# A ternary feed-forward layer whose down projection runs two tiles behind, with f32 transposes in a ring of three buffers

## The chip, the cores and the metric

The kernel runs on one core of one Trainium2 chip. The metric is the device time of the whole kernel in microseconds (us). The core has five engines that run side by side: PE (TensorE, matmuls; its weight loads are listed apart as PEld), DVE (VectorE), ACT (ScalarE), POOL (GpSimd) and SP (SyncE, which here only starts transfers). Each runs its own instructions in the order in which they are written and waits for others by semaphores. PE has two clock levels, 1.2 and 2.4 GHz; the profile gives the granted clock as a share of full speed.

## What is computed

Four layers, each added to x, on 2048 rows of 512 numbers: a masked attention, a ternary feed-forward layer, a second attention and a gated feed-forward layer. The change lies in the second:

```python
def _rmsnorm(x, g):
    return g * (x * jax.lax.rsqrt(jnp.mean(x * x, axis=-1, keepdims=True) + EPS))
def _act_quant(x):
    scale = 127.0 / jnp.clip(jnp.max(jnp.abs(x), axis=-1, keepdims=True), 0.0001, None)
    y = jnp.clip(jnp.round(x * scale), -128, 127) / scale
...
def _linear_bit(x, w, g):
    xq = _act_quant(_rmsnorm(x, g))
    wq = _ternary_quant(w)
    return jnp.einsum('bsd,od->bso', xq, wq)
swish = jax.nn.silu(_linear_bit(x, w1, g1))
x_v = _linear_bit(x, w2, g2)
h = swish * x_v
return _linear_bit(h, w3, g3)
...
x = x + _L0_ffn_ref(_layernorm(x, axis=-1), L0_ffn_w1, ...)
```

w1 and w2 lead from 512 to 2048 columns, w3 from 2048 back to 512.

## The kernel before

`build_ternary_ffn` starts at line 743. The three ternary matrices lie in SBUF in bf16 from the start of the stage. The 2048 rows are cut into 16 tiles of 128 (NT). The work on a tile has these parts, by the names in the code:

- **prepare** (DVE, lines 931 to 944): mean and variance of the tile's rows (`bn`, `mv`), `u` = (x - mean) times g1 and times g2, and the largest value of each (`amax`). POOL turns these into the scale factors `kx` and `dqx` in a chain of eleven small instructions (lines 844 to 862), each of which waits for the one before.
- **quantise** (line 946): DVE multiplies and rounds `u` by adding a large constant (`um`), takes the constant off again and writes bf16 (`xq`); PE transposes the eight 128x128 blocks into PSUM (`TX`, line 1024), ACT copies them to SBUF (`xqt`, line 894).
- **products** (PE, lines 1030 to 1040): for n from 0 to 3 four matmuls of 512 columns into `G` (w1) and four into `V` (w2), both with two buffers in PSUM. ACT takes silu of G (line 914), DVE multiplies it by V to `h` (`gate`, line 969), ACT squares and sums h (line 901), POOL multiplies h by g3 to `u3` (line 871), DVE takes its largest value (line 974). Then DVE reduces the four partial results (`red`) and POOL makes `k3` and `dq3` of them (lines 876 to 883).
- **h rounded** (ACT, line 907): one instruction over 2048 columns (`hm`); DVE writes it as bf16 (`hq`, line 985), PE transposes 16 blocks into `TH` (line 1046), ACT copies one half and DVE the other to `hqt` (lines 921 and 1004).
- **down** (PE, line 1057): 16 matmuls with w3 into `DN`; DVE scales them and adds them to x (`xr`, line 1011); SP stores the tile.

The order is written out by hand in `step(t, before, ahead)` on each engine. Step t does the products of tile t, the transposes and the down matmuls of tile t-1 (`before`), the quantise of tile t+1 and the prepare of tile t+2 (`ahead`). Steps 1 to 13 are one hardware loop (`Fori`), whose waits compare with register values. x is loaded twice per tile: into `xz` for prepare and into `xr` for the update, each a single buffer.

## Time and profile before

| | us |
|---|---|
| median of 3 runs | 1853.65 (1852.92 to 1854.41) |
| the profiled execution, its own time | 1850.29 |
| its span, first to last instruction | 1848.5 |
| ternary stage, first instruction to the next stage's first | 650.88 to 975.42 |

| engine | busy us of the span | share |
|---|---|---|
| PE | 1489.4 | 81% |
| DVE | 959.9 | 52% |
| ACT | 678.6 | 37% |
| POOL | 404.6 | 22% |

These shares are means over four stages with different limits, so they say little about the ternary stage. For that the profile is read by stretches of time (windows), by the timeline of one step, and by groups of equal instructions. In a timeline row the bracket gives how long the engine stood idle before the instruction and whose result ended that. The rows stand below, ahead of the prediction.

### The profile page before, as it was taken

The numbers are of one execution on the slowest core, as the hardware profiler recorded it, in microseconds if no ns is written. First come the engines' busy times: TensorE is split into PE (matmuls) and PEld (weight loads), VectorE is DVE, ScalarE is ACT, GpSimd is POOL, SyncE is SP. The second block draws the span as 40 slices with busy tenths as digits, with TensorE's granted clock in tenths as the row PEclk, the third lists the DMA queues.
The fourth block names the chain that finished last, engine by engine and source line by source line (L and its number), as shares of the span: only waits on it lengthen the run. The fifth ranks groups of instructions, "written<-read, shape, count | busy, mean of one in ns | idle before, by whom it ended". The sixth has DMA issues, their size and how long they took to land. (4 is left out here: it accounts for less than half of the span.)

```text
span 1848.5 us, 25537 instructions
## 1 busy us (share of the span) xinstructions
PE 1489.4 (81%) x9033; PEld 657.7 (36%) x9106; DVE 959.9 (52%) x1526; ACT 678.6 (37%) x1212; POOL 404.6 (22%) x502
## 2 busy tenths in 40 slices
PE   3568878877787747867672898899599999999998
PEld 2334534444343213333330122222144444444443
DVE  6544744646646358788853788888332032131220
ACT  2153444444434424544440566666322021121120
POOL 4210101101100046666642233342200000000000
PEclk8678988889888968888885899999799999999999
DMA  5524254253442121111113556453300100100100
GB/s 137 91 87 107 81 142 87 96 127 81 122 97 72 58 66 34 45 40 41 44 35 120 164 180 217 150 194 117 124 1 0 69 1 1 68 0 0 46 0 23
DMA packets 91704, 146.29 MB, mean 79 GB/s; under 512 B 7624, under 2 KB 48136, under 8 KB 90064
## 3 DMA queue, kind: packets, MB, share of 16 engines
q1 hardware_dynamic: 78816, 119.93, 22.9%
q10 hardware_dynamic: 12800, 25.17, 4.3%
q8 instruction: 58, 0.95, 0.2%
q14 instruction: 30, 0.25, 0.0%
HBM read 114.23 MB, written 30.83 MB: 78 GB/s over the span
## 5 line engine op out<-in xcount | busy, mean ns | idle before, releaser
L488 DVE TENSOR_REDUCE a_negmax<-a_psX 128x4 f32<-128x1024 f32 x128 | 149.8, 1216 | 170.9 <-PE a_psX L682 170.3
L1349 DVE TENSOR_REDUCE c_negmax<-c_psA 128x1 f32<-128x512 f32 x256 | 163.9, 673 | 60.4 <-PE c_psA L1420 58.2
L373 ACT ACTIVATE a_probs<-a_psB 128x512 f32<-128x512 f32 x256 | 138.5, 593 | 145.6 <-PE a_psB L692 145.5
L1653 PE MATMUL d_psGU<-d_zt_lo,last_w_hi 128*128 128x512 bf16 x501 | 189.9, 379 | 2.2 <-DVE d_zt_lo L1607 1.7
L1653 PE MATMUL d_psGU<-d_zt_hi,last_w_hi 128*128 128x512 bf16 x502 | 190.3, 379 | 0.6
L1653 PE MATMUL d_psGU<-d_zt_hi,last_w_lo 128*128 128x512 bf16 x501 | 189.9, 379 | 0.6
L1576 ACT ACTIVATE d_silu<-d_psGU 128x512 f32<-128x512 f32 x64 | 38.2, 597 | 378.2 <-PE d_psGU L1653 378.2
L692 PE MATMUL a_psB<-a_qs,a_ks 115*128 115x256 bf16 x512 | 138.7, 401 | 45.7 <-ACT a_probs L373 40.2
L1295 ACT ACTIVATE c_probs<-c_psB 128x512 f32<-128x512 f32 x256 | 142.2, 595 | 90.8 <-PE c_psB L1433 88.6
L1618 DVE TENSOR_TENSOR d_h<-d_psGU,d_silu 128x512 f32<-128x512 f32 x64 | 44.2, 691 | 236.4 <-PE d_psGU L1653 236.4
L1420 PE MATMUL c_psA<-c_ks,c_qs 96*128 96x512 bf16 x256 | 105.1, 412 | 50.6 <-DMA c_qs<-q_scr 29.1
L1057 PE MATMUL b_psD<-ternary,b_hq_t 128*128 128x512 bf16 x254 | 85.9, 513 | 53.0 <-ACT b_hq_t L921 53.0
L682 PE MATMUL a_psX<-a_ks,a_qs 113*128 113x256 bf16 x512 | 79.9, 297 | 52.3 <-DVE a_negmax L488 29.8
L1433 PE MATMUL c_psB<-c_qs,c_ks 98*128 98x512 bf16 x256 | 95.0, 389 | 7.7 <-ACT c_probs L1295 7.0
L1663 PE MATMUL d_psD<-last_w_hi,d_h_lo 128*128 128x512 bf16 x252 | 95.5, 379 | 0.3
L1663 PE MATMUL d_psD<-last_w_hi,d_h_hi 128*128 128x512 bf16 x251 | 95.1, 379 | 0.4
L1663 PE MATMUL d_psD<-last_w_lo,d_h_hi 128*128 128x512 bf16 x249 | 94.4, 379 | 0.2
L266 POOL TENSOR_SCALAR a_ve<-a_mv 128x2 f32<-128x2 f32 x8 | 1.9, 232 | 418.1 <-DVE a_mv L421 418.1
L871 POOL TENSOR_TENSOR b_u<-b_h,b_g 128x512 f32<-128x512 f32 x64 | 84.4, 1333 | 40.6 <-DVE b_h L969 37.5
L1630 DVE TENSOR_TENSOR d_xr<-d_psD,d_xr 128x512 f32<-128x512 f32 x16 | 10.4, 690 | 150.6 <-PE d_psD L1663 113.2
L692 PEld LDWEIGHTS a_psB<-a_qs,a_ks 115*128 115x128 bf16 x512 | 43.6, 107 | 125.8 <-ACT a_probs L373 74.9
L705 PE MATMUL a_psOS<-a_probs,a_v 128*32 128x256 f32 x1024 | 85.7, 462 | 0.0
(207 smaller groups left out, 2641.9 us busy)
## 6 DMA issues: line engine op xcount, KB each, us to landing
a_tern_stage<-in_w ACTq DMA_DIRECT2D x32, 768.0 KB, 7.5
c_weight_stage<-in_w_last SPq DMA_DIRECT2D x8, 1536.0 KB, 8.7
a_ks<-k_scr SPq DMA_DIRECT2D x24, 256.0 KB
a_qs<-q_scr SPq DMA_DIRECT2D x24, 256.0 KB
c_ks<-k_scr SPq DMA_DIRECT2D x48, 128.0 KB, 2.6
c_qs<-q_scr SPq DMA_DIRECT2D x48, 128.0 KB, 3.0
a_xz<-in_x SPq DMA_DIRECT2D x8, 512.0 KB, 18.5
a_ctx<-in_ctx_t SPq DMA_DIRECT2D x8, 512.0 KB, 12.7
```

What stands on the lines that cost most here:

```text
L373: act.activation(pr[:, e % 4, :, jj * P:(jj + 1) * P].rearrange("p r (a i) -> p a r i", a=2), B[:, u % 2, :].rearrange("p (a r i) -> p a r ...
L488: v.tensor_reduce(negm[:, u, :], X[:, 2 * (u % 2):2 * (u % 2) + 2, :].rearrange("p a (j k) -> p (a j) k", k=SEQ), AX.X, ALU.max, negate=Tr ...
L692: last = pe.matmul(B[:, u % 2, a * SEQ:(a + 1) * SEQ], ks[par][0:K_ALL, j, grp, kt * P:(kt + 1) * P], qflat[par][0:K_ALL, SHARE * grp * SE ...
L705: pe.matmul(OS[32 * r:32 * r + 32, c % 2, 0, :], v1[par][:, kt, grp, :], pr[:, (2 * grp + kt) % 4, r, :], start=(grp % 2 == 0 and kt == 0) ...
L871: g.tensor_tensor(u3[:, n, :], h[:, n, :], g3[:, n * 512:(n + 1) * 512], ALU.mult)\
L1057: last = pe.matmul(DN[:], hqt[:, i, :], w3[:, i, :], start=(i == 0), stop=(i == FC - 1))
L1295: act.activation(pr[:, e % 2, j, :], B[:, j % 2, :], ACT.Exp, scale=HD1 ** -0.5)\
L1349: v.tensor_reduce(negm[:, u:u + 1], A[:, u % 2, :], AX.X, ALU.max, negate=True)\
L1420: pe.matmul(A[:, u % 2, :], qs[par][0:K1, head, (u % QT) * P:(u % QT + 1) * P], ks[par][0:K1, head, :], start=True, stop=True).then_inc(s[ ...
L1433: pe.matmul(B[:, j % 2, :], ks[par][0:K1 + 2, head, kt * P:(kt + 1) * P], qs[par][0:K1 + 2, head, :], start=True, stop=True).then_inc(s["s ...
L1653: last = pe.matmul(GU[:, 2 * up + i % 2, :], wgu[wh][:, k, o:o + P], zt[zh][:, k, :], start=(k == 0 and j == 0), stop=(k == DC - 1 and j = ...
L1663: last = pe.matmul(DN[:, t, :], ht[hh][:, i, t * P:(t + 1) * P], wd[wh][:, i, :], start=(i == 0 and j == 0), stop=(i == FC - 1 and j == 2))
```

## The change

All of it is in `build_ternary_ffn`.

- The down matmuls of a tile come two steps after its products instead of one, in four groups of four that stand between the product groups. Step t does products of t, transposes and down of t-2.
- There is no bf16 copy before a transpose. ACT rounds x (`rounded`) and h (`scaled`, in two halves of 1024 columns); PE transposes the f32 values with the large constant still on them, four blocks into one PSUM bank of 512 f32. Three such banks (`T`) form a ring for the chunks of tiles t-2 (four of h) and t+1 (two of x) in the order `CHUNKS`. The constant is taken off where a chunk is read out (`take`): even chunks by ACT, odd ones by DVE with a tensor-scalar instruction.
- x has one ring of ten tiles (`b_x`) that serves prepare and update, so each tile is loaded once. SP loads tiles 0 and 1 ahead of g1 and g2, and waits for a store's landing before it loads the tile ten further on.
- prepare runs four tiles ahead in rings of four; `u` for g1 and g2 is one instruction of 1024 columns, and so is `amax`. POOL makes `kx` and `dqx` for two tiles at once, 13 instructions in every even step, in four parts between its products with g3.
- DVE takes the largest values of u3 in two reduces of 1024 columns instead of four of 512.
- `dqx_now` and `dq3_now`, the two small copies, are gone. The hardware loop is gone too: 19 steps are written out, with constant waits.

The diff, cut to its core:

```diff
     NF = FF // 512
+    RING, RU = 10, 4
+
+
+    CHUNKS = [("x", 0, 0), ("x", 0, 1)]
+    for t in range(NT + 2):
+        CHUNKS += [("h", t - 2, i) for i in range(2) if t >= 2]
+        CHUNKS += [("x", t + 1, j) for j in range(2) if t + 1 < NT]
+        CHUNKS += [("h", t - 2, i) for i in range(2, NF) if t >= 2]
+    AT = {c: k for k, c in enumerate(CHUNKS)}
+    TAKEN = {c: (c[2] % 2, sum(1 for d in CHUNKS[:k + 1] if d[2] % 2 == c[2] % 2)) for k, c in enumerate(CHUNKS)}
...
+            def rounded(t):
+                act.wait_ge(s["kx_done"], 2 * (t // 2 + 1))
+                act.wait_ge(s["u_done"], t + 1)
+                if t >= 2:
+                    act.wait_ge(s["filled"], AT["x", t - 2, 1] + 1)
+                for j in range(2):
+                    act.activation(um[:, t % 2, j, :], u[:, t % RU, j, :], ACT.Identity, scale=kx[:, t % RU, j:j + 1],
+                                   bias=keep["round"][:]).then_inc(s["um_done"], 1)
+
+            def take(kind, t, i):
+                if (kind, t, i) not in AT:
+                    return
+                act.wait_ge(s["filled"], AT[kind, t, i] + 1)
+                dst = xqt[:, t % 2, i, :] if kind == "x" else hqt[:, t % 2, i * 512:(i + 1) * 512]
+                act.activation(dst, T[:, AT[kind, t, i] % 3, :], ACT.Identity, bias=unround[:]).then_inc(s["taken_act"], 1)
...
+            def scaled(t, half):
+                if half == 0:
+                    act.wait_ge(s["k3_done"], 2 * (t + 1))
+                    act.wait_ge(s["u3_done"], NF * (t + 1))
+                    if t >= 2:
+                        act.wait_ge(s["filled"], AT["h", t - 2, NF - 1] + 1)
+                own = slice(half * FF // 2, (half + 1) * FF // 2)
+                act.activation(hm[:, t % 2, own], u3[:, t % 2].rearrange("p n d -> p (n d)")[:, own], ACT.Identity,
+                               scale=k3[:, t % 2:t % 2 + 1], bias=keep["round"][:]).then_inc(s["hm_done"], 1)
+
+            act.wait_ge(s["init"], 2)
+            rounded(0)
+            take("x", 0, 0)
+            for t in range(NT + 2):
+                now = t < NT
+                if now:
+                    gate(t, 0)
+                take("h", t - 2, 0)
+                if t + 1 < NT:
+                    rounded(t + 1)
+                if now:
+                    squares(t, 0)
+                    gate(t, 1)
+                    squares(t, 1)
+                    gate(t, 2)
+                take("x", t + 1, 0)
+                if 1 <= t <= NT:
+                    scaled(t - 1, 0)
+                if now:
+                    squares(t, 2)
+                    gate(t, 3)
+                take("h", t - 2, 2)
+                if 1 <= t <= NT:
+                    scaled(t - 1, 1)
+                if now:
+                    squares(t, 3)
...
-            def quantise(t):
-                dve.wait_ge(s["kx_done"], t + 1)
-                for j in range(2):
-                    v.tensor_scalar(um[:, j, :], u[:, j, :], kx[:, j:j + 1], ROUND, ALU.mult, ALU.add)\
-                        .then_inc(s["xq_rounded"], 1)
-                need(dve, s["tx_done"], t)
-                for j in range(2):
-                    dve.wait_ge(s["xq_rounded"], 2 * t + j + 1)
-                    v.tensor_scalar(xq[:, j, :], um[:, j, :], ROUND, 127.0, ALU.subtract, ALU.min)\
-                        .then_inc(s["xq_done"], 1)
...
+            for t in range(NT + 3):
+                now = t < NT
+                ahead = prepare(t + 4) if t + 4 < NT else iter(())
+                if t >= 3:
+                    update(t - 3)
+                if now:
+                    gate(t, 0)
+                if 1 <= t <= NT:
+                    largest(t - 1, 1)
+                    reduced(t - 1)
+                next(ahead, None)
+                if now:
+                    gate(t, 1)
+                take("h", t - 2, 1)
+                next(ahead, None)
+                if now:
+                    gate(t, 2)
+                take("x", t + 1, 1)
+                next(ahead, None)
+                if now:
+                    largest(t, 0)
+                    gate(t, 3)
+                take("h", t - 2, 3)
 
...
+            def transposed(kind, t, i):
+                if (kind, t, i) not in AT:
+                    return
+                k = AT[kind, t, i]
+                if k >= 3:
+                    engine, count = TAKEN[CHUNKS[k - 3]]
+                    pe.wait_ge(taken[engine], count)
+                if kind == "x":
+                    pe.wait_ge(s["um_done"], 2 * t + i + 1)
+                    src = um[:, t % 2, i, :]
+                else:
+                    pe.wait_ge(s["hm_done"], 2 * t + i // 2 + 1)
+                    src = hm[:, t % 2, i * 512:(i + 1) * 512]
+                for c in range(DC):
+                    last = pe.transpose(T[:, k % 3, c * P:(c + 1) * P], src[:, c * P:(c + 1) * P], keep["ident"][:])
+                last.then_inc(s["filled"], 1)
...
+            def down(t, i):
+                if ("h", t, i) not in AT:
+                    return
+                engine, count = TAKEN["h", t, i]
+                pe.wait_ge(taken[engine], count)
+                if i == 0:
+                    need(pe, s["x_updated"], t)
+                for k in range(4 * i, 4 * i + 4):
+                    last = pe.matmul(DN[:], hqt[:, t % 2, k * P:(k + 1) * P], w3[:, k, :], start=(k == 0), stop=(k == FC - 1))
+                if i == NF - 1:
                     last.then_inc(s["d_done"], 1)
 
...
+            for t in range(NT + 2):
+                for n in range(NF):
+                    if t < NT:
+                        product(t, n, 0, G, "silu_done", "g_done")
+                        product(t, n, 1, V, "h_done", "v_done")
+                    if n:
+                        down(t - 2, n - 1)
+                    transposed("h", t - 2, n)
+                    if n == 1:
+                        for j in range(2):
+                            transposed("x", t + 1, j)
+                down(t - 2, NF - 1)
 
 
```

PE before, from the transposes of h in the loop's body to the end of the body (`psTH` and `psTX` are the two transposes, `psD` the down matmuls, in brackets what a row waits for):

```order
L1046 MATMUL b_psTH<-ident_bf,b_hq 128x128 [waits b_hqt_dve,b_hqt_act]
L1046 MATMUL b_psTH<-ident_bf,b_hq 128x128 x15
L1020 ISA
L1024 MATMUL b_psTX<-ident_bf,b_xq 128x128 [waits b_xqt_done,b_xq_done]
L1024 MATMUL b_psTX<-ident_bf,b_xq 128x128 x7
L1057 MATMUL b_psD<-ternary,b_hq_t 128x512 [waits b_x_updated,b_hqt_act]
L1057 MATMUL b_psD<-ternary,b_hq_t 128x512 x7
L1057 MATMUL b_psD<-ternary,b_hq_t 128x512 [waits b_hqt_dve]
L1057 MATMUL b_psD<-ternary,b_hq_t 128x512 x7
```

PE after, the second half of a steady step and the first groups of the next:

```order
L1114 MATMUL b_psD<-ternary,b_hq_t 128x512 [waits b_taken_act]
L1114 MATMUL b_psD<-ternary,b_hq_t 128x512 x3
L1093 MATMUL b_psT<-ident,b_h_rounded 128x128 [waits b_hm_done,b_taken_act]
L1093 MATMUL b_psT<-ident,b_h_rounded 128x128 x3
L1114 MATMUL b_psD<-ternary,b_hq_t 128x512 [waits b_taken_dve]
L1114 MATMUL b_psD<-ternary,b_hq_t 128x512 x3
L1102 MATMUL b_psG<-ternary,b_xq_t 128x512 [waits b_silu_done,b_taken_act]
L1102 MATMUL b_psG<-ternary,b_xq_t 128x512 x3
L1102 MATMUL b_psV<-ternary,b_xq_t 128x512 [waits b_h_done,b_taken_dve]
L1102 MATMUL b_psV<-ternary,b_xq_t 128x512 x3
```

Where all 16 transposes of h, the 8 of x and the 16 down matmuls stood in a row at the end, groups of four now stand between the products; the last down group stands directly behind the last transposes of h, and the one before it behind the last V group.

ACT before, one turn of the loop's body:

```order
L907 ACTIVATE b_h_rounded<-b_u3,round_bias,b_k3 128x2048
L914 ACTIVATE b_silu<-b_psG,b_dqx_now 128x512 x2
L901 ACTIVATE b_sq,b_ssq<-b_h 128x512
L914 ACTIVATE b_silu<-b_psG,b_dqx_now 128x512
L901 ACTIVATE b_sq,b_ssq<-b_h 128x512
L914 ACTIVATE b_silu<-b_psG,b_dqx_now 128x512
L901 ACTIVATE b_sq,b_ssq<-b_h 128x512 x2
L921 ACTIVATE b_hq_t<-b_psTH 128x1024
L894 ACTIVATE b_xq_t<-b_psTX 128x1024
```

ACT after, the end of one steady step and the start of the next (it begins with silu of n = 2):

```order
L932 ACTIVATE b_silu<-b_psG,b_dqx 128x512
L927 ACTIVATE b_xq_t<-b_psT,b_minus_round 128x512
L950 ACTIVATE b_h_rounded<-b_u3,round_bias,b_k3 128x1024
L940 ACTIVATE b_sq,b_ssq<-b_h 128x512
L932 ACTIVATE b_silu<-b_psG,b_dqx 128x512
L927 ACTIVATE b_hq_t<-b_psT,b_minus_round 128x512
L950 ACTIVATE b_h_rounded<-b_u3,round_bias,b_k3 128x1024
L940 ACTIVATE b_sq,b_ssq<-b_h 128x512
L932 ACTIVATE b_silu<-b_psG,b_dqx 128x512
L927 ACTIVATE b_hq_t<-b_psT,b_minus_round 128x512
L919 ACTIVATE b_u_rounded<-b_u,round_bias,b_kx 128x512 x2
L940 ACTIVATE b_sq,b_ssq<-b_h 128x512
```

ACT has gained the two roundings of x, three takes of 512 columns stand where two copies of 1024 were, and the rounding of h is split and stands among the squares; the take of h's chunk 2 is behind silu of n = 3.

## Rows read from the trace of the kernel before

**Rows 1.** Windows of the ternary stage: stretch, its length, busy us per engine (instructions), clock, DMA.
```profile
core 0: us, PE busy (x) PEld busy (x) DVE busy (x) ACT busy (x) POOL busy (x), PEclk, DMA share, GB/s
...
650.88:670.13 19.25, 1.04 (x8) 0.77 (x8) 7.17 (x15) 1.02 (x1) 5.74 (x14) 0.50 0.32 110
...
705.72:948.14 242.42, 180.53 (x923) 84.67 (x935) 193.30 (x319) 121.78 (x196) 156.52 (x270) 0.87 0.14 41
...
948.14:975.42 27.28, 18.13 (x95) 8.86 (x94) 11.85 (x20) 9.32 (x15) 7.99 (x10) 0.87 0.14 49
```

**Rows 2.** Timeline, one steady step: start, length, engine, line, operation, out<-in [idle before <-releaser].
```profile
819.14 0.69 ACT L914 ACTIVATE b_silu<-b_psG,b_dqx_now 128x512 f32<-128x512 f32 x1 [0.46 <-DVE b_dqx_now L961]
...
820.11 0.75 DVE L969 SCALAR_TENSOR_TENSOR b_h<-b_psV,b_dqx_now,b_silu 128x512 f32<-128x512 f32 x1 [1.16 <-ACT b_silu L914]
...
820.55 0.69 ACT L914 ACTIVATE b_silu<-b_psG,b_dqx_now 128x512 f32<-128x512 f32 x1 [0.72 <-PE b_psG L1033]
...
821.13 0.62 ACT L901 ACTIVATE b_sq<-b_h 128x512 f32<-128x512 f32 x1
...
821.65 0.19 ACT L901 ACTIVATION_READ_ACCUMULATOR b_sq<-b_h 128x1 f32 x1
...
824.66 1.06 PE L1046 MATMUL b_psTH<-ident_bf,b_hq 128*128 128x128 bf16 x16
...
826.52 0.62 PE L1024 MATMUL b_psTX<-ident_bf,b_xq 128*128 128x128 bf16 x8 [0.80 <-DVE b_xq L954]
...
827.75 0.63 ACT L901 ACTIVATE b_sq<-b_h 128x512 f32<-128x512 f32 x1 [3.06 <-DVE b_h L969]
...
830.69 5.03 PE L1057 MATMUL b_psD<-ternary,b_hq_t 128*128 128x512 bf16 x16 [3.55 <-ACT b_hq_t L921]
```

**Rows 3.** Groups by line and form, ternary stage: count | busy us, mean ns | idle before.
```profile
L969 DVE SCALAR_TENSOR_TENSOR b_h<-b_psV,b_dqx_now,b_silu 128x512 f32<-128x512 f32 x64 | 47.5, 742 | 22.2 <-ACT b_silu L914 20.0 <-PE b_psV L1038 2.2
...
L907 ACT ACTIVATE b_h_rounded<-b_u,round_bias,b_k 128x2048 f32<-128x2048 f32 x16 | 33.5, 2093 | 55.7 <-POOL b_dq L883 55.7
...
L871 POOL TENSOR_TENSOR b_u<-b_h,b_g 128x512 f32<-128x512 f32 x64 | 84.4, 1333 | 40.6 <-DVE b_h L969 37.5 <-issue 2.9
...
L939 DVE SCALAR_TENSOR_TENSOR b_u<-b_xz,b_mv,b_g 128x512 f32<-128x512 f32 x32 | 22.6, 749 | 0.6
...
L985 DVE TENSOR_SCALAR b_hq<-b_h_rounded 128x2048 bf16<-128x2048 f32 x16 | 19.5, 1217 | 0.6 <-ACT b_h_rounded L907 0.6
```

**Rows 4.** Timeline of PE in the last stage: f32 transposes, then bf16 matmuls.
```profile
1675.48 1.94 PE L1642 MATMUL d_psGU<-ident,d_z 128*128 128x128 f32 x16 [0.88 <-DVE d_h L1618]
1677.25 0.38 PE L1663 MATMUL d_psD<-last_w_hi,d_h_hi 128*128 128x512 bf16 x1
1677.47 0.38 PE L1663 MATMUL d_psD<-last_w_hi,d_h_lo 128*128 128x512 bf16 x1
```

**Rows 5.** Groups by line and form, whole span: nearest forms to the new instructions.
```profile
L488 DVE TENSOR_REDUCE a_negmax<-a_psX 128x4 f32<-128x1024 f32 x128 | 149.8, 1216 | 170.9 <-PE a_psX L682 170.3
...
L1571 ACT ACTIVATE d_h_hi<-d_h 128x512 bf16<-128x512 f32 x64 | 39.8, 622 | 8.8 <-DVE d_h L1618 8.8
...
L1564 ACT ACTIVATE d_zt_hi<-d_psGU 128x512 bf16<-128x512 f32 x16 | 8.5, 602 | 23.2 <-PE d_psGU L1642 22.8
...
L1270 ACT ACTIVATE c_ctx_hi<-c_ctx 128x1024 bf16<-128x1024 f32 x8 | 8.4, 1056 | 31.7 <-DMA c_ctx<-in_ctx 24.9 <-DMA k_scr<-c_ctx_lo 6.8
```

**Rows 6.** Windows after a stop of PE, and without one (columns as in 1).
```profile
830.69:834.40 3.71, 3.71 (x11) 1.42 (x12) 3.43 (x9) 0.86 (x1) 1.96 (x4) 0.61 0.00 0
...
955.90:957.75 1.85, 0.00 (x2) 0.12 (x3) 1.12 (x2) 1.56 (x3) 1.25 (x1) 1.00 0.00 0
...
967.12:969.90 2.78, 2.78 (x7) 1.04 (x8) 0.00 (x0) 0.00 (x0) 0.00 (x0) 0.50 0.00 0
```

**Rows 7.** Timeline of POOL: first and last link of an undisturbed h chain.
```profile
958.28 0.19 POOL L876 TENSOR_SCALAR b_scalars<-b_red 128x1 f32<-128x1 f32 x1 [1.13 <-DVE b_red L1001]
...
960.48 0.19 POOL L883 TENSOR_TENSOR b_dq<-b_scalars,level 128x1 f32<-128x1 f32 x1
```

**Rows 8.** Timeline of DVE: the first tile of the stage.
```profile
660.17 0.69 DVE L934 BATCH_NORM_STATS2 b_bn<-b_xz 128x6 f32<-128x512 f32 x1 [20.33 <-DMA b_xz<-x]
```

More of the change, by code:

```diff
@@ L789, in build_ternary_ffn @@
         s = {n: ctx.enter_context(nc.semaphore("b_" + n)) for n in names}
+        loaded = [s[f"x_loaded{i}"] for i in range(4)]
+        taken = [s["taken_act"], s["taken_dve"]]
         block = ctx.enter_context(nc.Block())
@@ L836, in _ @@
+            for t in range(4, RING):
+                load(t)
+            for t in range(NT):
+                sp.wait_ge(s["x_updated"], t + 1)
+                sp.dma_start(x_out[t * P:(t + 1) * P, :], xt[:, t % RING, :]).then_inc(s["stored"], DMA)
+                if t + RING < NT:
+                    sp.wait_ge(s["stored"], (t + 1) * DMA)
+                    load(t + RING)
             sp.wait_ge(s["stored"], NT * DMA)
@@ L890, in _ @@
+            pool.wait_ge(s["g3_loaded"], DMA)
+            for t in range(NT + 1):
+                chain = iter(())
+                if t % 2 == 0 and t + 2 < NT:
+                    chain = x_chain(t + 2)
+                if t >= 1:
+                    h_chain(t - 1)
+                if t < NT:
+                    for n in range(NF):
+                        gated(t, n)
+                        next(chain, None)
         @block.scalar
         def _(act):
-            def quantise(t):
-                act.wait_ge(s["tx_done"], t + 1)
-                act.activation(xqt[:], TX[:], ACT.Copy).then_inc(s["xqt_done"], 1)
@@ new lines, in prepare @@
+                yield
+                dve.wait_ge(s["mv_done"], t + 1)
+                if t == 0:
+                    dve.wait_ge(s["g12_loaded"], 2 * DMA)
+                v.scalar_tensor_tensor(out=u[:, r], in0=xt[:, t % RING, :].rearrange("p (o d) -> p o d", o=1)
+                                       .broadcast_to([P, 2, D]), scalar=mv[:, r, 0:1], in1=g12[:],
+                                       op0=ALU.subtract, op1=ALU.mult).then_inc(s["u_done"], 1)
+                yield
+                dve.wait_ge(s["u_done"], t + 1)
@@ new lines, in gate @@
+            def gate(t, n):
+                dve.wait_ge(s["v_done"], NF * t + n + 1)
+                dve.wait_ge(s["silu_done"], NF * t + n + 1)
+                if t:
+                    dve.wait_ge(s["u3_done"], NF * (t - 1) + n + 1)
+                    dve.wait_ge(s["ssq_done"], NF * (t - 1) + n + 1)
+                v.scalar_tensor_tensor(out=h[:, n, :], in0=V[:, n % 2, :], scalar=dqx[:, t % RU, 1:2],
+                                       in1=silu[:, n % 2, :], op0=ALU.mult, op1=ALU.mult).then_inc(s["h_done"], 1)
@@ new lines, in update @@
+            def update(t):
+                dve.wait_ge(s["d_done"], t + 1)
+                dve.wait_ge(s["k3_done"], 2 * (t + 1))
+                v.scalar_tensor_tensor(out=xt[:, t % RING, :], in0=DN[:], scalar=dq3[:, t % 4:t % 4 + 1],
+                                       in1=xt[:, t % RING, :], op0=ALU.mult, op1=ALU.add).then_inc(s["x_updated"], 1)
+            for t in range(2):
+                for _part in prepare(t):
+                    pass
+            take("x", 0, 1)
+            for t in range(2, 4):
+                for _part in prepare(t):
+                    pass
@@ new lines, in product @@
+            def product(t, n, j, out, freed, done):
+                engine, count = TAKEN["x", t, j]
+                if n == 0:
+                    pe.wait_ge(taken[engine], count)
+                need(pe, s[freed], NF * t + n - 1)
+                for k in range(DC):
+                    last = pe.matmul(out[:, n % 2, :], xqt[:, t % 2, j, k * P:(k + 1) * P],
+                                     w12[j][:, k, n * 512:(n + 1) * 512], start=(k == 0), stop=(k == DC - 1))
+                last.then_inc(s[done], 1)
```

386 lines of the change are left out of this document (145 added, 241 removed).

## The prediction

> **What bounds the kernel now.** I read the stretches first. The ternary stage runs from 650.88 to 975.42 us, 324.5 of the span's 1848.5; everything outside it is untouched code, so only these 324.5 us can move, unless a neighbour's start moves with them. Between the first update of x and the fourteenth there are 13 periods in 242.4 us, **18.65 us per tile**, and no engine is full in them: PE 180.5 (74%), DVE 193.3 (80%), POOL 156.5, ACT 121.8 [rows 1]. So a loop through several engines sets the period. The timeline of one step shows where: PE waits 0.80 before the transposes of the next x (for DVE's rounding), and then 3.55 before the down matmuls, for ACT's copy of the transposed h. ACT makes that copy only after its last two squares, and those had waited 3.06 for the gate on DVE [rows 2]. After that stop most of the down matmuls go at the lower clock (granted 0.61 of full over 3.7 us [rows 6]; the 16 take 5.03 [rows 2] where 16 x 0.2155 is 3.45). That is the shape to undo: everything of one tile (transposes, copy, down) stands in one row at the step's end and each link waits for another engine.
>
> **What the change does to each engine, per tile.** *PE:* 48 matmuls of 512 columns at 0.2155 apart [rows 4] are 10.34, as before. The 24 transposes become f32: 16 of them take 1677.25 - 1675.48 = 1.77, 0.11 each [rows 4], against 1.06/16 = 0.066 in bf16 [rows 2]. So 2.65, 1.06 more than now, all on PE's own path. Sum 13.0.
> *DVE* loses the two roundings of x, their conversions and that of h. It gets three readings of 512 f32 columns out of PSUM by a tensor-scalar instruction. The same instruction out of SBUF takes 1.217 for 2048 columns [rows 3], which would put 512 at 0.3 to 0.4. The rows that read f32 out of PSUM are slower: half of the 1.216 reduce is 0.61 [rows 5], and the gate takes 0.742 [rows 3]. Bounds 0.3 and 0.74; I take 0.68, since the new source is the gate's. (The Trainium skill, "VectorE: DVE Perf Modes", section "Why PSUM operands drop a tier", says that an f32 operand in PSUM allows no doubled rate. By it 0.68 stands; by the row out of SBUF the period below would be 0.3 shorter and the sum 1807.) The double u (1024 columns) lies between 0.749 and twice that [rows 3]; 1.3 taken. Gates 2.97, two reduces of 1024 2.43, amax 1.22, u 1.3, takes 2.04, statistics 0.87, update 0.75, small ones 0.3: 11.9.
> *ACT* gets x's rounding, 2 of 512. A plain copy is 0.622 for 512 and 1.056 for 1024 [rows 5], so 1.92 for 2048; the rounding of h with its two column operands is 2.093 [rows 3], 0.17 more. So 0.80 each, and 1.23 for a half of h. The takes (PSUM, one column operand): 0.602 without it [rows 5], 0.69 for silu, which has one [rows 2]: 0.69. ACT instructions that wait for nothing start about 0.1 before the last ends (silu 820.55, 0.69 long, square at 821.13), and a square with its accumulator read takes 0.71 [rows 2]. Starts are then 0.59 (silu, take), 0.71, 0.70, 1.13 apart: 2.36 + 1.77 + 2.84 + 1.40 + 2.26 = 10.6.
> *POOL:* four products of 1.333 [rows 3], the chain of h, 958.28 to 960.67, 2.4 [rows 7], and 13 links for x per pair of tiles, about 5.5 by the same lengths: 10.5 on average, 13.2 in an even step, nothing in an odd one. Hidden while the period is above that.
> *SP:* each update of x releases a store, and behind its landing on the same queue stands the load of the tile ten further on, whose first reader comes six periods later, some 90 us. Cost nothing; without that cover it would be a landing, 2 to 3 us. No row of the steady step waits for a DMA today either, so there is nothing to gain.
>
> **Walk through one steady step**, zero at its first G matmul. PE without waits: G0 V0 to 1.72, transposes h0 to 2.16, G1 V1 to 3.88, down0 to 4.74, h1 to 5.18, x0 x1 to 6.06, G2 V2 to 7.78, down1 to 8.64, h2 to 9.08, G3 V3 to 10.80, down2 to 11.66, h3 to 12.10, down3 to 12.96. A reader can start 0.2 after a group's last slot (16 transposes end 0.17 after the next matmul began [rows 4]).
> ACT in its order: silu0 1.06; take h0 must wait for PE, 2.36; roundings 2.95 and 3.65; square0 4.35; silu1 5.05 to 5.75. DVE's gate1 starts 0.28 after that (819.14 + 0.69 to 820.11 [rows 2]), 6.0 to 6.8, so square1 waits to 6.8, silu2 7.5, take x0 8.1, first half of h 8.7, square2 9.8, silu3 10.55, take h2 11.15 to 11.85. **down2 stood ready at 10.80 and starts at 11.9.** h3's transposes end 13.2, DVE's take of them runs 13.4 to 14.1, and **down3, which stands directly behind its own transposes, starts at 14.15** and ends at 15.0. So two waits stay, 1.1 and 0.95, and the period is **15.0**. DVE and POOL keep up: gate0 is out at 2.7, the reduce and red at 4.2, POOL's h chain by 6.6, before ACT wants k3 at 8.7; the squares end near 13.7, before silu0 of the next step at 16.1.
> Neither wait should cost clock: through 1.85 us without a matmul the clock stayed at 1.00, while after 3.55 us it was 0.61 [rows 6, 2].
>
> **Ends.** Before the first G now: 19.25 us [rows 1], DVE waiting for x until 660.17 [rows 8]. Now x0, x1, g1, g2 (1.0 MB instead of 1.75) come first, and 7.3 us of transfer shrink to about 4, but the first chain needs statistics and maxima of two tiles (DVE 5.8): rounding at 666, G0 near 668.7, a gain of 1.4 (0 to 6). Step 0: gate0 stands behind the take and the preparation of tiles 2 and 3 (6.6 us) on DVE, so it runs at 676; the rest of ACT's row, 9.8, brings the next silu0 to 685.8, and step 1, without h's takes, to 696.7. Zero of step 2: 695.6. Fourteen periods: 905.6.
> Then tiles 14 and 15, groups of 0.44 and 0.86 with a take of about 0.95 between each, and once a take of h2 queued behind the rounding of tile 15 (1.8): 9.8 and 8.9, update and store 3.3, together 22.1 against 975.42 - 948.14 = 27.3 for two tiles and a half now [rows 1]. PE is idle half of that, which no row shows; full clock (the 1.85 us row) adds 0, the lower one, 0.50 in the last matmuls of now [rows 6], adds 10. I take 5. End of the stage: 905.6 + 22.1 + 5 = 932.7.
> **Sum:** 975.4 - 932.7 = 42.7 less. The profiled execution's own time, 1850.3, becomes 1807.6; the median shown is 3.4 above it, so **1811**.
>
> **Rivals.**
> *B, ACT is ahead.* If its lengths come out 10% shorter, down2 doesn't wait and only down3's 0.95 stays: 13.95 per tile, 14 x 1.05 = 15 less, 1796. For: most terms are upper ones. Against: the row of fifteen instructions has one wait for DVE inside it that doesn't shrink.
> *C, waits that the walk missed.* POOL's even steps: 5.3 + 3.3 (the h chain when DVE is busy) + 7 is 15.6, u3 comes late to the reduce ahead of gate3 on DVE, and the take of h3 behind it; or ACT 10% longer. 16 to 17 per tile, 1825 to 1839.
> *D, slower than before.* PE runs at the lower clock in the steady part. Full, that is 13.0 us more per tile; the gain of 42.7 is used up at 3.05 us per tile, so from 23% of PE's work at 1.2 GHz on. All of it would give 1993; at 30%, 1866. Against: 16 f32 transposes in a row had a granted clock of 1.00 around them and the matmul behind them came at 0.22 spacing [rows 4], and today's full stretches between long stops.
> The Trainium skill ("TensorE: Matmul & The Clock Gate", "Part 4: PE-mode transpose") says that a transpose doesn't count as busy for the clock gate as a matmul does. By it 2.65 of the 13.0 would weigh as idle. Rows 4 are after a long busy stretch and can't refute it.
> *E, no gain,* the period is bound by something like DVE at its present load: I see nothing for it, since DVE loses 3 to 6 us.
>
> **Chances.** Forecast (14.5 to 15.7 per tile) 0.50, B 0.15, C 0.27, D 0.06, E 0.02. A measurement of this kernel can tell about 0.2%. Faster 0.92, same 0.02, slower 0.06. The range goes from B with a tail at full clock, 1791, to C's upper end with a little lower clock, 1842.
>
> **What would show it.** Waits of PE before down2 (for ACT's take) and down3 (for DVE's), about 1 us each, none above 2; periods between updates of x of 15.0; f32 transposes at 0.11; DVE near 12 us and ACT near 11 per tile; granted clock in the steady part above 0.95. It is wrong if PE waits mainly at a G or V (then ACT or DVE is the bound), if stops exceed 3 us, or if the takes out of PSUM are far from 0.68.

## The result, and the profile after

| | before | after |
|---|---|---|
| median, us | 1853.68 (1852.92 to 1854.41, 4 runs) | **1811.55** (1808.03 to 1813.51, 4 runs) |
| ratio | | **0.9771, 95% interval 0.9754 to 0.9788** |
| profiled execution, own time / span | 1850.3 / 1848.5 | 1808.03 / 1806.2 |
| ternary stage | 650.88 to 975.42 | 650.26 to 930.24 |

The forecast was 1811.0 with a range of 1791 to 1842. The windows of the changed kernel's ternary stage, cut as [rows 1] are (before the first G; from the first update of x on; the tail), and below them two tiles of the steady part:

```profile
core 0: us, PE busy (x) PEld busy (x) DVE busy (x) ACT busy (x) POOL busy (x), PEclk, DMA share, GB/s
650.26:670.57 20.31, 1.90 (x9) 1.57 (x9) 6.67 (x8) 2.25 (x4) 5.74 (x15) 0.50 0.57 207
715.95:907.93 191.98, 172.19 (x928) 94.13 (x927) 136.31 (x191) 136.94 (x244) 125.74 (x200) 1.00 0.08 27
907.93:930.24 22.31, 11.96 (x65) 6.33 (x63) 6.36 (x10) 5.01 (x6) 2.04 (x6) 0.97 0.09 35
790.72:820.64 29.92, 26.66 (x145) 14.62 (x144) 23.25 (x33) 21.41 (x38) 20.52 (x33) 1.00 0.08 27
```

PE was busy 74% of the steady part and is now busy 89 to 90% of it, and the granted clock rose from 0.87 to 1.00. Per tile the last row gives 13.3 us on PE, 11.6 on DVE, 10.7 on ACT, 10.3 on POOL in a period of 14.96. DVE's update of x, once per tile (timeline; start, length, ..., [idle before <-releaser]; three of sixteen):

```profile
805.72 0.75 DVE L1043 SCALAR_TENSOR_TENSOR b_x<-b_psD,b_dq,b_x 128x512 f32<-128x512 f32 x1 [1.13 <-PE b_psD L1114]
820.64 0.75 DVE L1043 SCALAR_TENSOR_TENSOR b_x<-b_psD,b_dq,b_x 128x512 f32<-128x512 f32 x1 [1.13 <-PE b_psD L1114]
835.64 0.75 DVE L1043 SCALAR_TENSOR_TENSOR b_x<-b_psD,b_dq,b_x 128x512 f32<-128x512 f32 x1 [1.13 <-PE b_psD L1114]
```

The first is at 715.95; the next nine follow 14.93 and 15.00 apart in turn, three more 14.6 apart (no later tile is left to prepare), then 13.74, 9.93 and 9.02. Of PE's rows in a steady step only two have a wait in them (timeline of PE, the end of one step):

```profile
800.47 1.03 PE L1102 MATMUL b_psV<-ternary,b_xq_t 128*128 128x512 bf16 x4
802.19 1.04 PE L1114 MATMUL b_psD<-ternary,b_hq_t 128*128 128x512 bf16 x4 [0.69 <-ACT b_hq_t L927]
803.06 0.60 PE L1093 MATMUL b_psT<-ident,b_h_rounded 128*128 128x128 f32 x4
804.65 1.04 PE L1114 MATMUL b_psD<-ternary,b_hq_t 128*128 128x512 bf16 x4 [0.98 <-DVE b_hq_t L1013]
```

Down group 2 waits for ACT's take and down group 3 for DVE's. Between 740 and 880 the weight loads of down matmuls stood 11.9 us for ACT (10 times) and 11.0 us for DVE (10 times), 1.2 and 1.1 each. The groups of instructions over 648 to 935 us (count | busy us, mean ns | idle before), where a term of the prediction had to be bounded from both sides:

```profile
L1022 DVE SCALAR_TENSOR_TENSOR b_h<-b_psV,b_dqx,b_silu 128x512 f32<-128x512 f32 x64 | 47.7, 746 | 38.8 <-PE b_psV L1102 21.8 <-ACT b_silu L932 16.9
L950 ACT ACTIVATE b_h_rounded<-b_u,round_bias,b_k 128x1024 f32<-128x1024 f32 x32 | 39.6, 1237 | 3.6 <-POOL b_dq L884 3.6
L999 DVE SCALAR_TENSOR_TENSOR b_u<-b_x,b_mv,b_g 128x1024 f32<-128x1024 f32 x16 | 25.4, 1586 | 2.8 <-DMA b_g<-in_g 2.7
L919 ACT ACTIVATE b_u_rounded<-b_u,round_bias,b_kx 128x512 f32<-128x512 f32 x32 | 24.2, 805 | 40.9 <-POOLq L863 40.9
L1013 DVE TENSOR_SCALAR b_hq_t<-b_psT 128x512 bf16<-128x512 f32 x32 | 21.9, 685 | 15.5 <-PE b_psT L1093 15.1
L927 ACT ACTIVATE b_hq_t<-b_psT,b_minus_round 128x512 bf16<-128x512 f32 x32 | 21.9, 684 | 16.5 <-PE b_psT L1093 16.5
```

### The profile page after: what moved, and what is told of

Read it like the earlier page. It is cut to its first block and busy times, and to the rows that moved or that the text cites. A ratio compares the mean times of both kernels' runs of the same rounds, so it can differ in the third digit from the quotient of the medians.

```text
span 1806.2 us, 24378 instructions
## 1 busy us (share of the span) xinstructions
PE 1488.1 (82%) x9106; PEld 671.2 (37%) x9106; DVE 904.6 (50%) x1382; ACT 701.6 (39%) x1276; POOL 371.0 (21%) x431
## 3 DMA queue, kind: packets, MB, share of 16 engines
q8 instruction: 65, 1.06, 0.3%
## 5 line engine op out<-in xcount | busy, mean ns | idle before, releaser
L1724 PE MATMUL d_psGU<-d_zt_hi,last_w_hi 128*128 128x512 bf16 x512 | 194.1, 379 | 1.4 <-DVE d_zt_lo L1678 1.4
L1724 PE MATMUL d_psGU<-d_zt_lo,last_w_hi 128*128 128x512 bf16 x512 | 194.0, 379 | 0.0
L1724 PE MATMUL d_psGU<-d_zt_hi,last_w_lo 128*128 128x512 bf16 x512 | 194.0, 379 | 0.0
L1114 PE MATMUL b_psD<-ternary,b_hq_t 128*128 128x512 bf16 x256 | 66.1, 381 | 30.8 <-DVE b_hq_t L1013 16.3
```

What stands on the lines that cost most here:

```text
L1724: last = pe.matmul(GU[:, 2 * up + i % 2, :], wgu[wh][:, k, o:o + P], zt[zh][:, k, :], start=(k == 0 and j == 0), stop=(k == DC - 1 and j = ...
```

## The experiments

Each edit is shown short. All are measured against the kernel before, on the same chip in the same stretch of runs (its median there was 1851.9 to 1852.9), so ratios are the safer comparison across groups. "Period" is the distance between DVE's updates of x.

### Are the two waits before the down groups what keeps the period at 15?

**e1, the take of h's chunk 2 earlier on ACT** (from the changed kernel):

```
 if 1 <= t <= NT:
     scaled(t - 1, 0)
+take("h", t - 2, 2)
 if now:
     squares(t, 2)
     gate(t, 3)
-take("h", t - 2, 2)
```

> ACT's take of h's chunk 2 stands two instructions earlier, directly behind the first half of the rounding of h. Theory (the period is ACT's row up to that take, plus PE's down2, last transposes, DVE's take and down3): the take ends at 10.5 of the walk instead of 11.85, PE no longer waits before down2 at 10.8, and only the wait before down3 stays: 13.95 per tile instead of 14.9, fourteen times, 1811.5 - 14 = about 1797. Rival (ACT as a whole, or DVE, is the bound): the wait only moves, to a G, V or another take, and the time stays within 4 us of 1811.

Measured: 1807.52 (1806.36 to 1812.55), ratio 0.9765 (0.9741 to 0.9789). The rival: the medians lie 4 us apart, but the ratios (0.9765 and 0.9771) can't be told apart, and the mean period of nine steady steps went from 14.96 to 14.85. Of PE's waits one is left, about twice as long (two steps in a row; in the changed kernel it was 0.98 and 0.78):

```profile
805.34 1.04 PE L1114 MATMUL b_psD<-ternary,b_hq_t 128*128 128x512 bf16 x4 [1.84 <-DVE b_hq_t L1013]
820.08 1.04 PE L1114 MATMUL b_psD<-ternary,b_hq_t 128*128 128x512 bf16 x4 [1.58 <-DVE b_hq_t L1013]
```

Down2 no longer waits, and what it saved is waited off before down3. ACT's row and DVE's row ran about equally late; with ACT moved away DVE is found right behind it.

**e2, the last down group one step later**, behind the first transposes of h of the next step, and DVE's update of x moved behind the two small reductions:

```
                     if n:
                         down(t - 2, n - 1)
                     transposed("h", t - 2, n)
+                    if n == 0:
+                        down(t - 3, NF - 1)
...
-                down(t - 2, NF - 1)
+            down(NT - 1, NF - 1)
```

> down3 of a tile stands in the next step, behind the first transposes there, and DVE's update of x behind the small reduces. Theory: DVE's take of chunk 3 is then covered, PE goes from the last transposes straight to the next G, and the wait before down2 stays: 13.2 to 13.4 per tile, 14 x 1.6 = 22 less, about 1789. Rival (ACT's wait before down2 grows by what the other wait gives back, since ACT's row of instructions has no room left): 14.3 or more per tile, above 1802.

Measured: 1801.83 (1799.7 to 1805.06), ratio 0.9731 (0.971 to 0.9753), most periods 14.2 to 14.3. That is at the rival's edge (above 1802, 14.3 or more) and far from the theory's 1789: down3's wait is gone, but down2's stays (0.49 and 0.97 us in two steps) and in one of them a new one of 0.37 stands before down0, for the update.

**e3, both edits.**

> Both edits. Theory: PE has no wait left and is the bound with its own 13.0 per tile (48 matmuls at 0.2155 and 24 f32 transposes at 0.11): 14 x 1.9 = 27 less, about 1784. Rival (ACT or DVE takes over before PE is full): ACT's 10.6 and its two waits for PE and DVE inside the row make 12.3, DVE 11.9 and its waits for silu about as much, so 13.5 to 14 per tile with PE waiting at a G or V, 1790 to 1798.

Measured: 1797.1 (1796.59 to 1802.1), ratio 0.9709 (0.9685 to 0.9733), period about 14.1, and 13.2 to 13.4 only in the steps where nothing is left to prepare. As the rival said, DVE takes over before PE is full, though the wait stands before down0, for the update, and not at a G or V. PE's waits between 785 and 819:

```profile
790.98 1.02 PE L1114 MATMUL b_psD<-ternary,b_hq_t 128*128 128x512 bf16 x4 [0.80 <-DVE b_x L1043]
805.17 1.02 PE L1114 MATMUL b_psD<-ternary,b_hq_t 128*128 128x512 bf16 x4 [1.05 <-DVE b_x L1043]
819.21 1.02 PE L1114 MATMUL b_psD<-ternary,b_hq_t 128*128 128x512 bf16 x4 [0.90 <-DVE b_x L1043]
```

### Do f32 transposes lower the clock?

**e4, e3 with each transpose of h done twice** into the same place.

> As e3_both, with each of the 16 transposes of h per tile done twice (the second overwrites the first with the same values). Theory: where PE is the bound each costs its 0.11, so 16 x 0.11 = 1.77 more per tile than e3, about 28 us in 16 tiles, and the granted clock stays at 1.00 in the steady part. Rival (transposes do not count as work for the clock): with 4.4 of 14.7 us per tile in transposes the clock falls in the steady part, matmuls come 0.43 apart in stretches, and the time is more than 40 us above e3.

Measured: 1813.0 (1811.58 to 1814.41, 2 runs), ratio 0.9786 (0.9759 to 0.9812), period 14.73, where PE's 13.0 and the 1.77 make 14.77. Windows of two tiles, first e3, then e4:

```profile
790.09:818.31 28.22, 26.37 (x145) 14.73 (x144) 23.64 (x34) 21.18 (x39) 19.57 (x33) 1.00 0.08 29
```

```profile
793.14:822.59 29.45, 29.45 (x178) 18.36 (x176) 22.44 (x34) 21.51 (x39) 20.57 (x33) 1.00 0.09 28
```

4.4 of 14.7 us per tile are now transposes, and the granted clock is 1.00 all the same: the rival is out. The time rose by 16, not by the theory's 28: the 1.77 us first filled the 0.9 of waiting that e3 still had per tile. PE is busy 29.45 of 29.45 us.

### How much of the gain is the loop, and how much the second tile of distance?

**e5, the kernel before with its hardware loop written out:**

```
-            with engine.Fori(1, NT - 2) as t:
+            for t in range(1, NT - 2):
```

> The kernel before with one edit: the hardware loop over the steady steps of the ternary stage is written out as straight code, nothing else moves. It asks how much of the 42 us belongs to the loop that the change also removed (its waits against registers and its branch). Theory (the gain is the order on the PE row; the loop costs at most the gaps at its edge, 0.5 to 0.9 us a step): 1840 to 1847, so no more than 13 us of the 42, and the updates of x still 17.7 to 18.3 us apart. Rival (the loop's register waits are the larger part of the gain): 1830 or less.

Measured: 1834.28 (1828.22 to 1839.91), ratio 0.991 (0.9878 to 0.9943), period 16.95. So 17.6 of the 42 us, more than the theory and less than the rival. PE still stands 3.61 us before its down matmuls there, as before (3.55). What went is its wait before the transposes of the next x. In the kernel before, that wait is 0.80 in one step and 1.8 to 1.9 in the next, and the periods alternate with it, 17.5 to 18.2 and 19.6 to 19.8; [rows 2] are from a short step. In e5 the wait is gone and the first ten periods are 16.94 or 16.95 (PE in the kernel before, two steps; then e5):

```profile
808.01 0.62 PE L1024 MATMUL b_psTX<-ident_bf,b_xq 128*128 128x128 bf16 x8 [1.94 <-DVE b_xq L954]
...
826.52 0.62 PE L1024 MATMUL b_psTX<-ident_bf,b_xq 128*128 128x128 bf16 x8 [0.80 <-DVE b_xq L954]
```

```profile
797.95 0.61 PE L1024 MATMUL b_psTX<-ident_bf,b_xq 128*128 128x128 bf16 x8
```

From the first transpose of h to the first of x PE takes 2.99 and 1.86 in these two steps, and 0.89 in e5. That is 1.5 of the 1.7 us per tile; the stretch from the first down matmul to the next G (5.58 and 4.86, 4.93 in e5) makes the rest. Two rows show why DVE's bf16 copy of x comes earlier. DVE's two roundings and two conversions of x took 1.96 + 1.82 in the step of [rows 2] and take 2.39 + 0.75 in e5, where the conversions no longer stand beside POOL's products. And POOL's chain of small instructions, which makes the scales that DVE's roundings wait for, runs faster (kernel before, in the loop; then e5):

```profile
817.64 0.19 POOL L850 TENSOR_TENSOR b_scalars<-b_scalars 128x1 f32<-128x1 f32 x1 [0.18 <-POOL b_scalars L849]
818.01 0.19 POOL L851 TENSOR_TENSOR b_scalars<-b_scalars,b_mv 128x1 f32<-128x1 f32 x1 [0.18 <-POOL b_scalars L850]
```

```profile
806.58 0.20 POOL L850 TENSOR_TENSOR b_scalars<-b_scalars 128x1 f32<-128x1 f32 x1
806.86 0.19 POOL L851 TENSOR_TENSOR b_scalars<-b_scalars,b_mv 128x1 f32<-128x1 f32 x1
```

The links start 0.37 to 0.39 apart in the loop and 0.28 apart without it; ahead of its loop the kernel before runs the same two links (663.05 and 663.32) 0.27 apart. What in the loop causes the gap no run shows. ACT's rounding of h (L907), which waits for POOL's other chain, idles 2.77 us before it, where it idled 3.55 in the loop's steps.

**e6, the changed kernel with h only one tile behind:** all transposes and down groups of tile t - 1 stand at the end of step t, and the takes move with them. So the edit also takes these groups out from between the products.

```
-                    if n:
-                        down(t - 2, n - 1)
-                    transposed("h", t - 2, n)
...
-                down(t - 2, NF - 1)
+                transposed("h", t - 1, 0)
+                transposed("h", t - 1, 1)
+                down(t - 1, 0)
+                transposed("h", t - 1, 2)
+                down(t - 1, 1)
+                transposed("h", t - 1, 3)
+                down(t - 1, 2)
+                down(t - 1, 3)
```

> The changed kernel with the h transposes and the down matmuls only one tile behind instead of two: all four transposes of h and the four down groups of tile t-1 stand at the end of step t, the takes likewise; one step fewer at the end. f32 transposes, the ring and the halves of the rounding stay. Theory (two behind is worth the distance between the chain h -> squares -> POOL -> rounding and its use, but at the step's end most of that distance is there already): period 16.1, that is 1.2 more over some 13 periods, less 8 for the shorter tail: 1818 to 1826. Rival (two behind is where the gain is: with one behind PE stands at each transpose as in the kernel before): period 18 or more, 1840 or above.

Measured: 1838.24 (1833.09 to 1846.27, 7 runs), ratio 0.9939 (0.9915 to 0.9962). Neither number: periods of 15.6 to 19.2, 17.1 on average over the first twelve. The theory's 16.1 is there in three of them; most others lose more. PE in a step of 16.13 (first two rows) and in the next, of 17.45:

```profile
799.19 1.06 PE L1092 MATMUL b_psT<-ident,b_h_rounded 128*128 128x128 f32 x8 [0.96 <-ACT b_h_rounded L949]
801.99 1.04 PE L1113 MATMUL b_psD<-ternary,b_hq_t 128*128 128x512 bf16 x4 [1.74 <-ACT b_hq_t L926]
...
818.54 1.49 PE L1113 MATMUL b_psD<-ternary,b_hq_t 128*128 128x512 bf16 x3 [2.14 <-ACT b_hq_t L926]
819.82 1.06 PE L1092 MATMUL b_psT<-ident,b_h_rounded 128*128 128x128 f32 x4
```

After the longer stop (0.96 and 2.14 us within 4) PE runs slower: four f32 transposes take 1.06 where they take 0.60 elsewhere. With one tile of distance, all other parts of the change together are worth no more than the written-out loop alone (1838 against 1834). The second tile, together with the places between the products that it opens, is worth the other 27 us; no run separates the two.

### What stands behind PE's last slack?

**e7, e3 with the update of x directly behind gate 0** instead of behind largest and the reductions.

> The kernel of e3 with one line moved: VectorE's update of x(t-3) stands directly behind gate 0 instead of behind the second half's largest and the two small reductions. In e3 down matmul 0 waits 0.80 and 1.05 us in each step for that update. Theory (with that wait gone PE is all that is left): period 13.1 to 13.3 in place of 14.1, 12 periods: 1783 to 1788. Rival (largest, and with it POOL's chain for h and the gates behind it, come 0.75 later, and in every second step ACT stands 2.2 us for POOL's kx; the wait comes back before gate products or transposes): less than 5 us gained, 1792 or above.

Measured: 1798.65 (1797.64 to 1802.0), ratio 0.972 (0.9703 to 0.9738), periods 13.74 and 15.23 in turn: the rival. The wait for the update is gone, and in every second step ACT stands 3 us for POOL:

```profile
805.97 1.52 ACT L919 ACTIVATE b_u_rounded<-b_u,round_bias,b_kx 128x512 f32<-128x512 f32 x2 [2.98 <-POOLq L863]
```

**e8, e3 with another beginning:** VectorE prepares tiles 2 and 3 ahead of its take of x(0), and POOL makes their scales before gate 0.

```
+            for t in range(2, 4):
+                for _part in prepare(t):
+                    pass
             take("x", 0, 1)
-            for t in range(2, 4):
-                for _part in prepare(t):
-                    pass
...
+            for _part in x_chain(2):
+                pass
...
-                if t % 2 == 0 and t + 2 < NT:
+                if t % 2 == 0 and 4 <= t + 2 < NT:
```

> The kernel of e3 with the beginning of the stage reordered: VectorE prepares tiles 2 and 3 before its take of x(0) instead of behind it, and POOL computes their scales in its idle time before gate 0 instead of between the gates of step 0. In e3 gate 0 of tile 0 starts at 678.29 though its product is there at 673.2, and PE stands 3.57 us at 691.58 for the rounding of x(2), then runs 3 groups at about half clock. Theory (both stand on the path): 5 us from the first and 2 to 5 from the second, 1787 to 1790. Rival (the wait is only handed on, since step 1 has POOL's chain for h on its path anyway): 1794 or above.

Measured: 1789.51 (1788.28 to 1789.98), ratio 0.9664 (0.9647 to 0.968). The theory: the first update of x is at 711.13 instead of 718.53 and all later ones keep their distances.

**e9, e8 with POOL's chain for x spread** over the odd and the even step:

```
-                chain = iter(())
-                if t % 2 == 0 and 4 <= t + 2 < NT:
-                    chain = x_chain(t + 2)
+                if t % 2 == 1 and t + 3 < NT:
+                    chain = x_chain(t + 3)
...
-                        next(chain, None)
+                        if n == 0 or n == 2 - (t + 1) % 2:
+                            next(chain, None)
```

> The kernel of e8 with POOL's chain for the scales of two x tiles spread over two steps: its first two parts stand in the odd step before (where POOL had no such chain), its last two behind the first and second gated product of the even step, instead of all four in the even step. In e3 and e7 every second step is the longer one, and in it ACT stands 2.2 to 3.0 us for POOL's kx and VectorE up to 0.9 us for POOL's product. Theory (POOL's uneven load is what keeps the step from PE's 13.0): the two kinds of step become alike, period 13.2 to 13.5 in place of 14.1: 1779 to 1783. Rival (the chain in the odd step delays that step's chain for h and its products as much as it did in the even one, so the loss only changes sides): the mean period stays above 13.9, 1787 or above.

Measured: **1781.49** (1780.73 to 1785.56), ratio **0.9619** (0.9596 to 0.9642), the best of all and as the theory said. The periods are 13.16 or 13.17 (once 13.52), and the timeline of PE from 790 to 822 us has no wait in it; between 740 and 880 PE's waits for other engines come to 1.0 us. Windows of two stretches of 28.5 us:

```profile
740.00:768.50 28.50, 27.94 (x155) 16.02 (x157) 25.47 (x35) 22.01 (x40) 22.09 (x37) 1.00 0.13 41
768.50:797.00 28.50, 28.30 (x155) 16.00 (x156) 25.77 (x36) 23.42 (x41) 22.37 (x37) 1.00 0.10 35
```

**e10, e9 with e7's edit on top.**

> The kernel of e9 with e7's edit on top: VectorE's update directly behind gate 0. In e7 that edit took the wait before down matmul 0 away and gave it back in the longer step, where POOL was late. Theory (with POOL evened out the edit pays what it should have paid in e7): period 13.0 to 13.2, PE busy all the time: 1776 to 1779, 2 to 5 below e9. Rival (largest later by 0.75 is as bad as the update later by 1.3): no better than e9, within 1.5 of it or above.

Measured: 1786.57 (1782.84 to 1791.36), ratio 0.9633 (0.9609 to 0.9656), periods 13.2 to 13.8: the rival. DVE then waits for POOL's product before its reduce, 15.0 us between 740 and 880, against 0.7 in e9. Largest comes later, POOL's chain for h comes later (it waits up to 4.2 us for the reduction, 2.9 in e9), and so do POOL's products. Its first update of x is also 4.6 us later (716.01 against 711.40). The intervals of the ratios of e9 and e10 overlap; that e10 is slower rests on one profiled execution of each.

### One part of the change undone

**e11, the gate's rounding whole again** (2048 columns at the first half's place).

```
-                own = slice(half * FF // 2, (half + 1) * FF // 2)
+                if half:
+                    return
+                own = slice(0, FF)
```

> The changed kernel with one of its parts undone: the gate's rounding on ACT is again one instruction over all 2048 columns (2.09 us, as in the kernel before) at the place of the first half, instead of 1.23 + 1.23. ACT has 0.37 us less to do per tile, but squares 2, gate 3 and the take of h chunk 2 stand 0.86 later behind it. Theory (that take is what down matmul 2 waits for, and that wait is on the path): period 15.5 to 15.8, 1819 to 1824. Rival (two tiles behind leaves ACT so much room that only its sum counts): within 4 us of the changed kernel or below it, 1815 or less.

Measured: 1824.37 (1821.02 to 1825.6), ratio 0.9839 (0.9816 to 0.9863), period 15.33 to 15.42, where the theory had 15.5 to 15.8 and 1819 to 1824. The take that down2 waits for stands behind the long instruction; ACT's row and then PE's of the same step:

```profile
802.73 2.09 ACT L952 ACTIVATE b_h_rounded<-b_u,round_bias,b_k 128x2048 f32<-128x2048 f32 x1
...
805.90 0.69 ACT L927 ACTIVATE b_hq_t<-b_psT,b_minus_round 128x512 bf16<-128x512 f32 x1
```

```profile
806.64 1.04 PE L1116 MATMUL b_psD<-ternary,b_hq_t 128*128 128x512 bf16 x4 [1.22 <-ACT b_hq_t L927]
```

So the halves are worth some 13 us here, though they cost ACT 0.37 us more per tile. But the mechanism of the theory gives only part of them, and that the time lies only 0.4 above its range is luck. From the first to the last update of x e11 takes 226.2 us and the changed kernel 211.1. Of these 15.1 us the first period makes 2.2, the next eight 3.3, the three with nothing left to prepare 2.2, and the last three periods 7.4 (40.1 against 32.7). There PE stops for 2.57 us, behind the long rounding of the last tile, and then runs at the lower clock to the end of the stage (0.52 from 923.45 to 942; PE, the stop and a later group):

```profile
923.45 1.09 PE L1116 MATMUL b_psD<-ternary,b_hq_t 128*128 128x512 bf16 x4 [2.57 <-ACT b_hq_t L927]
...
929.70 1.89 PE L1116 MATMUL b_psD<-ternary,b_hq_t 128*128 128x512 bf16 x4 [0.78 <-ACT b_hq_t L927]
```

## Why the prediction was right, point by point

**The frame held.** Only the ternary stage moved: 324.5 us became 280.0. What follows it, in the same code, took 875.96 instead of 873.08 us, and nearly all of the difference lies in the attention stage (359.66 us from the end of the ternary stage to the first f32 transposes of the last layer, 357.03 before). Every experiment, too, had 2 to 8 us more between its last update of x and its end than the kernel before, even e5 (3.0), whose only edit is the loop. These are single profiled executions, one of each kernel. I did not find out why.

**The terms.** The f32 transposes, 4 in 0.44 us, are 0.11 apart; takes out of PSUM 0.685 on DVE (0.68 predicted, between bounds of 0.3 and 0.74) and 0.684 on ACT (0.69); rounding of x 0.805 (0.80); half of h 1.237 (1.23). PE's sum was put at 13.0 and e9, where PE hardly ever stands, runs at 13.16. The 0.685 agrees with the Trainium skill ("VectorE: DVE Perf Modes", "Why PSUM operands drop a tier"), by which an f32 operand in PSUM allows no doubled rate. **One term was mis-sized:** the double u of 1024 columns, 1.3 in the sum, 1.586 on average. It takes 1.28 at the beginning, with POOL idle, and more where POOL's products run beside it (timeline of the changed kernel, DVE and POOL, two steps):

```profile
797.51 2.05 DVE L999 SCALAR_TENSOR_TENSOR b_u<-b_x,b_mv,b_g 128x1024 f32<-128x1024 f32 x1
...
812.96 1.61 DVE L999 SCALAR_TENSOR_TENSOR b_u<-b_x,b_mv,b_g 128x1024 f32<-128x1024 f32 x1
```

```profile
797.21 1.27 POOL L891 TENSOR_TENSOR b_u<-b_h,b_g 128x512 f32<-128x512 f32 x1
...
812.22 1.28 POOL L891 TENSOR_TENSOR b_u<-b_h,b_g 128x512 f32<-128x512 f32 x1
813.45 2.27 POOL L891 TENSOR_TENSOR b_u<-b_h,b_g 128x512 f32<-128x512 f32 x1
```

The first u starts 0.97 us before the product beside it ends and is 0.77 too long, the second 0.54 and 0.33. POOL pays in the same way: the product that starts at 813.45, while u has 1.12 us left to run, takes 2.27 instead of 1.27. In these rows the instruction that starts second loses most of the overlap. The Trainium skill ("GPSIMD Engine Reference", "1. Specifications") says that the two engines contend for SBUF where the VectorE instruction has two SBUF inputs; the trace agrees, and the sum of the prediction had no term for it. It did little harm in the changed kernel. In every second step DVE's take of h3 starts as soon as its transposes allow (down3 then waits 0.78); in the others it starts straight behind gate 3, 0.2 later (0.98), and the reduce ahead of that gate had waited 0.17 for a product of POOL.

**The walk** said: down2 waits 1.1 for ACT, down3 0.95 for DVE, period 15.0. Measured: 0.69 (1.2 at the weight load), 0.98, and 14.93 or 15.00; the walk put down2 at 11.9 and down3 at 14.15 from the first G, and in the step from 805.52 on they start at 11.8 and 14.0. Counted as in the walk, from start to start, the two waits are 0.86 and 1.15 in the step shown, 2.0 together where it had 2.05. e1 corrects the reading, too: taking ACT's wait away gave 0.1 us per tile where I then expected 1.0, since DVE's row was about as late as ACT's. The step that e1 speaks against is rival B's "down2 doesn't wait and only down3's 0.95 stays": down3's wait would have grown. What makes DVE's row late in e1 (POOL's product, the reduce ahead of gate 3, the take of h3 behind it) the prediction had named, but under rival C, as a price of longer steps, not as what stands behind ACT's wait.

**The clock.** "Neither wait should cost clock" held: 1.00 in the steady part, waits of 1 us included, where before it was 0.87 with stops of 3.55. e4 decides rival D as far as transposes go: 30% of PE's time in f32 transposes and the clock stays at its upper level of 2.4 GHz. The Trainium skill ("TensorE: Matmul & The Clock Gate", "Part 4: PE-mode transpose") says that transposes don't count as busy; here, between matmuls, no loss of clock from it can be seen.

**The ends were wrong twice, in opposite directions.** The walk put the end of step 2 at 710.6; the first update came at 715.95, 5 late. The first G was at 670.57 (668.7 predicted), because DVE's u waited 2.69 for the weights g, until 657.5. Then PE waited 3.58 for the rounding of x(2). ACT itself had stood 2.39 there for POOL's scales of that tile, and the walk, whose step 1 ran ACT's row without waits, did not have this. PE ran at half clock behind that stop (0.53 from 691 to 697):

```profile
691.37 1.94 PE L1093 MATMUL b_psT<-ident,b_u_rounded 128*128 128x128 f32 x8 [3.58 <-ACT b_u_rounded L919]
...
914.72 1.04 PE L1114 MATMUL b_psD<-ternary,b_hq_t 128*128 128x512 bf16 x4 [1.68 <-ACT b_hq_t L927]
```

The second row is the tail: its work was 22.3 us where the walk said 22.1, with the wait behind the rounding of tile 15 that it named, but the 5 us put on top for the clock did not come. PE idles half of the time there and the clock is 0.97. The risk was real: in e11 the same tail has a stop of 2.57 instead of 1.68 and goes on at the lower clock (0.52). Together: start +5.1, twelve periods of 14.87 instead of 15.0 −1.6, the shorter last step −1.3, clock of the tail −4.8, that is −2.6; and +2.9 in the untouched stages. The sum of 1807.6 for the profiled execution therefore met 1808.0 partly by luck: its own errors were 5 us each way. The 3.4 us from there to the median were carried over from the kernel before, and 3.5 came.

**What the prediction did not see** is that writing out the loop alone, in the order of before, gives 1.7 of the 3.7 us gained per tile (e5). It walked the new row from zero, so the total did not need that split; what the loop would cost in the new order no run shows. What points to it stood in the trace of before: an idle of 0.18 before nearly each link of POOL's chain, which the code without a loop doesn't have. Rival C took 3.3 us for the chain of h with DVE busy. Part of that belonged to the loop: in the changed kernel, with DVE busy, the chain takes 2.4 (794.73 to 797.13).

## What to carry to other kernels

Walk one steady step with measured start distances instead of adding up waits: it gave the period to 0.1 us, while removing one wait of about 1 us alone (e1) gave 0.1 us, since a second engine's row was as late. Distance between a result and its use (two tiles instead of one, and with it a place between the products) was worth more than everything else in this change, and once PE is nearly full, what is left sits in an engine that nobody looks at because its average is low: POOL's uneven steps cost 0.9 us per tile at 70% load. Costing a kernel whose hardware loop goes away, look for the small gaps between dependent links. Treat beginning and end as walks of their own: in e11 half of the loss stood in the last three periods.

## What the runs showed that I had not expected

- Dependent links on POOL: 0.28 apart in straight code, 0.37 to 0.39 in the hardware loop, and writing the loop out gives 17.6 us in the whole kernel (e5).
- DVE's u with both inputs in SBUF went from 1.28 to 2.05 us beside a product of POOL, and such a product from 1.27 to 2.27 when it started behind u; in e9, where POOL is busier, u took 1.99 on average in the steady part. DVE's reads out of PSUM (takes 0.68, gates 0.75) did not change.
- After stops of 3.6 us PE ran at half clock for about 5 us; in the tail, with stops of 0.8 to 1.7 us before every down group and PE busy half of the time, it kept 0.97. In e11's tail one stop of 2.57 us was enough for 0.52 to the end of the stage.
- Steps of two kinds: an engine that works for a pair of tiles in one of them sets periods of 13.74 and 15.23 in turn (e7), and both become 13.16 when its work is spread (e9).
